# Narrow attention layer with two 64-row TensorE tiles, two-bank maxima and one key tile a step

## The reference

```
xn = rmsnorm(x, norm_w)                      # over 256 channels
q = (xn @ wq).reshape(B, T, 16, 16)          # T = 2048
k = (cond @ wk).reshape(B, S, 4, 16)         # S = 1601
v = (cond @ wv).reshape(B, S, 4, 16)
scores = einsum('btgrd,bsgd->bgrts', qg, k) / 4
attn = softmax(scores, axis=-1)
out = einsum('bgrts,bsgd->btgrd', attn, v)
return x + out @ wo
```

## Time and profile before

| | before |
|---|---|
| median of three timed executions | 4600.92 us |
| span of the profiled execution | 4597.9 us |
| TensorE busy | 4495.0 us, 98% |
| VectorE busy | 3081.4 us, 67% |
| ScalarE busy | 2309.8 us, 50% |
| mean granted TensorE clock | 0.987 |
| narrow layer's heads, end of head 0 to end of head 15 | 1742.24 to 2359.99 us |

### The profile page before, as it was taken

How to read it: one execution, slowest core, us unless ns; L and a number is a source line. 1 busy time by engine, 2 the same in 40 slices (tenths; PEclk the granted TensorE clock), 3 DMA queues, 4 the chain that set the end, 5 groups by cost and what they waited for, 6 DMA issues and landing times.

```text
span 4597.9 us, 56871 instructions
## 1 busy us (share of the span) xinstructions
PE 4495.0 (98%) x20657; PEld 2841.8 (62%) x20657; DVE 3081.4 (67%) x5037; ACT 2309.8 (50%) x4121; POOL 2827.0 (61%) x1365
## 2 busy tenths in 40 slices
PE   8999999999999979999999999999999999999999
PEld 7888866666656545555556666666656656665664
DVE  3321467777777678777846777777767677777776
ACT  3222455554555436666655555555555545554553
POOL 0000368898889711111036988898884888898886
PEclk9999999999999979999999999999999999999999
DMA  4555832221222021011234222222216212222220
GB/s 151 180 187 166 283 86 63 68 69 45 67 64 52 13 39 16 12 15 16 57 97 123 67 59 53 64 69 49 56 45 223 63 37 67 64 69 53 59 48 29
DMA packets 124633, 349.68 MB, mean 76 GB/s; under 512 B 28085, under 2 KB 46005, under 8 KB 113338
## 3 DMA queue, kind: packets, MB, share of 16 engines
q1 hardware_dynamic: 124352, 346.04, 28.4%
HBM read 191.31 MB, written 120.31 MB: 68 GB/s over the span
## 4 chain that ended last, share of the span: by engine, by line
PE 92%; DVE 6%; issue 1%; DMA 1%; ACT 0%; SPq 0%; POOL 0%; DVEq 0%; ACTq 0%
PE ST L989 13%; PE SS L970 12%; PE ST L990 12%; PE OA L1000 12%; PE OB L1000 11%; PE ST L1134 5%; PE OA L1142 4%; PE SS L1120 3%; DVE acc L1581 3%; PE OB L1120 1%; PE SS L1009 1%; DVE mpart L1560 1%; PE ST L1065 1%; PE ST L1066 1%; PE ST L1067 1%
## 5 line engine op out<-in xcount | busy, mean ns | idle before, releaser
L870 POOL TENSOR_TENSOR acc<-acc,P 128x1024 f32<-128x1024 f32 x912 | 2216.6, 2460 | 299.5 <-DVE acc L1587 286.3
L1321 ACT ACTIVATE P<-ST 128x512 f32<-128x512 f32 (+1 forms) x2496 | 1463.7, 597 | 1260.8 <-PE ST L990 1117.5
L1560 DVE TENSOR_REDUCE mpart<-SS 128x1 f32<-128x400 f32 (+1 forms) x3072 | 1629.7, 570 | 669.7 <-PE SS L970 594.4
L989 PE MATMUL ST<-QX,KX 128*128 128x512 f32 (+1 forms) x2496 | 1024.2, 410 | 3.5 <-DMA QS<-mrow 1.7
L970 PE MATMUL SS<-KS,QS 68*128 68x400 f32 (+1 forms) x3072 | 977.6, 352 | 14.7 <-DMA QS<-stq 8.3
L990 PE MATMUL ST<-QS,KS 69*128 69x512 f32 (+1 forms) x2496 | 990.1, 397 | 0.0
L970 PEld LDWEIGHTS SS<-KS,QS 68*128 68x128 f32 x3072 | 583.9, 190 | 191.3 <-DVE xacc L1611 23.9
L989 PEld LDWEIGHTS ST<-QX,KX 128*128 128x128 f32 (+1 forms) x2496 | 463.9, 186 | 360.2 <-issue 272.8
L1000 PE MATMUL OA<-P,Vp 128*64 128x512 f32 (+1 forms) x2496 | 658.3, 606 | 0.0
L1000 PE MATMUL OB<-P,Vp 128*64 128x512 f32 (+1 forms) x2496 | 641.3, 592 | 0.0
L1420 ACT ACTIVATE PG<-ST 128x512 f32<-128x512 f32 (+1 forms) x832 | 426.3, 618 | 213.3 <-PE ST L1134 213.1
(11 more groups left out here) (250 smaller groups left out, 4492.3 us busy)
## 6 DMA issues: line engine op xcount, KB each, us to landing
q_parts<-stq SPq DMA_DIRECT2D x96, 512.0 KB, 5.2
QX<-q_parts SPq DMA_DIRECT2D x96, 512.0 KB, 11.2
KX<-k_parts SPq DMA_DIRECT2D x48, 801.0 KB, 9.1
QS<-q_parts SPq DMA_DIRECT2D x45, 512.0 KB
R<-R SPq DMA_DIRECT2D x360, 64.0 KB, 2.0
v_tiles<-sv SPq DMA_DIRECT2D x24, 832.0 KB, 6.5
Vp<-v_tiles SPq DMA_DIRECT2D x24, 832.0 KB, 7.1
k_parts<-skh SPq DMA_DIRECT2D x48, 400.5 KB, 4.9
```

Of the source, the lines that this page charges most:

```text
L870: gp.tensor_tensor(out, out, P[0:k, slot(H, t), q, :], ALU.add).then_inc(pool_a, 1)
L989: pe.matmul(bank, KX[H % 2][:, t * 128:t * 128 + k], QX[H % 2][:, q], start=True, stop=False)
L1321: act.activation(P[0:k, slot(H, t), j, :], ST[n % 3][0:k, :], ACT.Exp, scale=SCALE).then_inc(act_p, 1)
L1560: dve.tensor_reduce(mpart[H % 2][:, i // len(KCH), c:c + 1], SS[RING_AT["s", H, i] % 3][:, 0:w], AX.X, ALU.max).then_inc(dve_ss, 1)
```

## The change

Only the narrow layer changes, and the names of four PSUM banks (SS0 to SS2 and OA become one tensor `S4` of four adjacent banks).

- Three parts of 16 rows are stacked in place of four of 32: K is (hi, hi, lo), Q is (hi, lo, hi), so the product lo times lo is left out. That makes 48 rows (49 with the max row), which fit in a 64-row tile of the array. K stands twice, at partitions 0 and 64. Q is divided: query blocks 0 and 2 at partition 0, blocks 1 and 3 at partition 64.
- `group_s` makes two matmuls for one item, one in each 64-row tile, into two adjacent banks; `group_s_max` reads both in one instruction. A head has 32 such pairs. The ring now has two places of two banks.
- `group_scores` with even j uses the lower tile, with odd j the upper.
- A step is one key tile: four ST matmuls, in two halves w = 0 and 1, each followed by one or two maxima pairs, then the PV of one tile. There are 13 steps a head.
- The output projection has four items of two banks instead of eight of one, and one add of 1024 columns for each; PV accumulates in OB.

```diff
-MROW = 3 * QD + D1
+GROWS = 3 * D1
+HALF = 64
+GPAIRS = SUNITS // 2
+HP = HU // 2
+GROW = KT - 3
+def group_units(h, t):
+    if t + 1 < KT:
+        return [(0, t + 1, j) for j in range(JQ)]
+    return [(1, 0, j) for j in range(JQ)] if h + 1 < HEADS else []
+def group_pairs(h, t, w):
+    if t >= GROW:
+        v = w + JQ // 2 * (t - GROW)
+        return 2, (part(GPAIRS, v, HP) if h + 2 < HEADS else range(0))
+    v = JQ // 2 * t + w
+    if h + 1 >= HEADS:
+        return 1, range(0)
+    return 1, (part(GPAIRS, v, JQ // 2 * GROW) if h == 0 else part(GPAIRS, HP - JQ // 2 * GROW + v, HP))
+def group_takes_row(h, t, w):
+    return t == GROW and w == 0 and h + 1 < HEADS
+def group_takes_sums(h, t):
+    return t == 3 and h > 0
+def group_o_item(h, t, w):
+    return t if h % GROUPS == 1 and h > GROUPS and t < JQ and w == 0 else None
+def group_q_item(h, t, w):
+    return t if h % QHEADS == QHEADS - 2 and h + 2 < HEADS and t < JQ and w == 0 else None
...
         def wait_group_ring(eng, at):
-            if at < len(GS):
+            if at < 2:
                 return
-            kind, n, i = GRING[at - len(GS)]
+            kind, n, i = GRING[at - 2]
...
             def group_q(h):
-                stack(GQ[h % 3], words(Q4hi[q, :]), words(Q4lo[q, :]), (0, 1, 0, 1), D1, gd_q[h % 3])
+                for i, src in enumerate((Q4hi, Q4lo, Q4hi)):
+                    blocks = words(src[q, :]).rearrange("d (b u c) -> d b u c", b=2, u=2)
+                    for half in range(2):
+                        to = HALF * half + i * D1
+                        sp.dma_start(words(GQ[h % 3][to:to + D1, 0:NQ // 2]).rearrange("d (b c) -> d b c", b=2),
+                                     blocks[:, :, half, :]).then_inc(gd_q[h % 3], 16)
...
             def group_s(h, i):
-                pe.matmul(GS[at % 4][:, 0:w], GQ[h % 3][0:MROW, qt * 128:(qt + 1) * 128],
-                          KG[h % GROUPS][0:MROW, o:o + w], start=True, stop=True).then_inc(gpe_s, 1)
+                for half in range(2):
+                    k = slice(HALF * half, HALF * half + GROWS)
+                    last = pe.matmul(group_bank("s", h, i, half)[:, 0:w], GQ[h % 3][k, qt * 128:(qt + 1) * 128],
+                                     KG[h % GROUPS][k, o:o + w], start=True, stop=True)
+                last.then_inc(gpe_s, 1)
...
             def group_scores(h, t, j):
                 wait(pe, gact_p, n - 2)
-                pe.matmul(ST[n % 3][0:k, :], KG[h % GROUPS][0:MROW + 1, t * 128:t * 128 + k],
-                          GQ[h % 3][0:MROW + 1, j * 512:(j + 1) * 512], start=True, stop=True).then_inc(gpe_st, 1)
+                r = slice(HALF * (j % 2), HALF * (j % 2) + GROWS + 1)
+                pe.matmul(ST[n % 3][0:k, :], KG[h % GROUPS][r, t * 128:t * 128 + k],
+                          GQ[h % 3][r, j // 2 * 512:(j // 2 + 1) * 512], start=True, stop=True).then_inc(gpe_st, 1)
...
             def group_head(h):
-                for g in range(STEPS):
-                    for u, (on, t, j) in enumerate(units(h, g)):
-                        group_scores(h + on, t, j)
+                for t in range(KT):
+                    both = group_units(h, t)
+                    for w in range(len(both) // 2):
+                        for on, ts, j in both[2 * w:2 * w + 2]:
+                            group_scores(h + on, ts, j)
...
                         for i in tiles:
                             group_s(h + ahead, i)
-                    pe.wait_ge(gact_p, HU * h + JQ * (PV[g][-1] + 1))
-                    for t in PV[g]:
-                        group_values(h, t)
+                    pe.wait_ge(gact_p, HU * h + JQ * (t + 1))
+                    group_values(h, t)
...
             def group_s_max(h, i):
-                dve.tensor_reduce(mpart[h % 2][:, i // len(KCH), c:c + 1], GS[GRING_AT["s", h, i] % 4][:, 0:w],
+                dve.tensor_reduce(mpart[h % 2][:, qt:qt + 9:8, c:c + 1], group_banks("s", h, i)[:, :, 0:w],
                                   AX.X, ALU.max).then_inc(gdve_ss, 1)
```

More of the change, by code:

```diff
@@ L351, in attention_layers @@
         ST = [bank(f"ST{i}") for i in range(3)]
-        SS = [bank(f"SS{i}") for i in range(3)]
-        OA, OB = bank("OA"), bank("OB")
+        S4 = ctx.enter_context(nc.psum_tensor("S4", [128, 4, 512], F32))
+        OB = bank("OB")
+        SS, OA = [S4[:, i, :] for i in range(3)], S4[:, 3, :]
         OAB = [OA, OB]
         PB = ST + SS + [OA, OB]
-        GS = SS + [OB]
         GB = [ST[0], ST[1], OA, OB]
@@ L885, in group_layer @@
                 for k in KG:
[L886 to L889, removed]
+                    for half in range(2):
+                        gp.memset(words(k[HALF * half + QD:HALF * half + 2 * QD, :]), 1.0).then_inc(pool_ones, 1)
                 for h in range(HEADS):
@@ L1109, in group_project @@
                 for ct in range(CT):
-                    last = pe.matmul(GS[at % 4][:, :], gwq[:, ct, :], xq[:, ct, j * 512:(j + 1) * 512],
+                    last = pe.matmul(group_bank("q", rnd, j), gwq[:, ct, :], xq[:, ct, j * 512:(j + 1) * 512],
                                      start=ct == 0, stop=ct == CT - 1)
@@ L1162, in group_head @@
[L1162 to L1172 removed]
+                pe.wait_ge(gpool_on, 4 * GROUPS * rnd + 4 * (GROUPS - 1) + j + 1)
@@ new lines, in group_output @@
+                wait_group_ring(pe, GRING_AT["o", rnd, j])
+                for ct in range(CT):
+                    last = pe.matmul(group_bank("o", rnd, j, ct), gwo[:, ct * 128:(ct + 1) * 128],
+                                     On[:, j * 512:(j + 1) * 512], start=True, stop=True)
+                last.then_inc(gpe_o, 1)
+            def group_head(h):
+                for t in range(KT):
+                    both = group_units(h, t)
+                    for w in range(len(both) // 2):
+                        for on, ts, j in both[2 * w:2 * w + 2]:
+                            group_scores(h + on, ts, j)
+                        ahead, tiles = group_pairs(h, t, w)
+                        if group_takes_row(h, t, w):
+                            group_transpose_max(h + 1)
+                        if group_o_item(h, t, w) is not None:
+                            group_output(h // GROUPS - 1, group_o_item(h, t, w))
+                        if group_q_item(h, t, w) is not None:
+                            group_project(h // QHEADS + 1, group_q_item(h, t, w))
@@ L1204, in group_layer @@
                 group_sums(HEADS - 1)
-                for i in range(8):
-                    group_output(ROUNDS - 1, i)
+                for j in range(JQ):
+                    group_output(ROUNDS - 1, j)
             for l in range(BIG):
@@ L1445, in group_layer @@
                     group_hi(0, j)
-                for t in PV[0]:
-                    for j in range(JQ):
-                        group_exps(0, t, j)
+                for j in range(JQ):
+                    group_exps(0, 0, j)
                 for h in range(HEADS):
@@ L1731, in group_layer @@
                     group_lo(0, j)
-                for i in range(SUNITS):
+                for i in range(GPAIRS):
                     group_s_max(0, i)
@@ L1738, in group_layer @@
                 group_reciprocals(HEADS - 1)
-                for i in range(8):
-                    group_add(ROUNDS - 1, i)
-                    if i % 2 == 1 and i > 1:
-                        split_x(1, (i - 3) // 2)
+                for j in range(JQ):
+                    group_add(ROUNDS - 1, j)
+                    if j > 0:
+                        split_x(1, j - 1)
             for l in range(BIG):
```

163 lines of the change are left out of this document (76 added, 87 removed).

## The result

Four timed executions of the changed kernel have a median of 4707.09 us (4692.26 to 4710.44), the kernel before beside them 4600.43. The ratio on record, taken over single executions, is 1.0224, 95% interval 1.0211 to 1.0237 (that of the two medians is 1.0232): slower by 107 us. The forecast was 4650, with a range that ended at 4696. The profiled execution took 4706.08 us.

What follows compares the result with a forecast made beforehand. A closed loop (first exponential, last score matmul, maxima work, PV, first score matmul) was taken to bound the kernel. Terms of 34 + 10 + 1 + 4 - 1 + 1 = 49 us gave 4650 us, range 4576 to 4696.

Steps and rivals of the forecast that it cites:

- plain-head term: Heads 1 to 13 and most of 14: a plain head takes 42.2 us instead of 39.74, +34 us.
- Thirteen loops: In a plain head, thirteen one-tile steps replace seven: 2.98 us each, three 0.19 longer, 39.3 us a head.
- Ring waits and max row: In plain heads, two-place ring waits add 0.9 and 0.3 us, the late negated maximum at tile 9 adds 0.46.
- The pair: Two 64-row maxima matmuls together cost one matmul of 0.19 us; the upper end adds 3.0 us a head.
- rival 1: The two row tiles or their loads do not overlap: 3.0 us a head on top, 4692 us; chance 0.17.
- Output items: Heads 5, 9 and 13: two-bank items hold up pairs in the ring, 3.4 to 3.6 us a head, +10 us.
- The query head: Head 6: its query items work like output items, 10.2 us against 9.2, +1 us.
- Head 15: Last head, without pairs: two one-tile steps take 5.36 us against 5.49, -1 us.
- Beginning: First maxima pass at 1.2 GHz, +3 us for 32 pairs, and the first head's Q loads, 1: together +4 us.
- Rival 2: In the steps: no ring waits, and half the output term, 4621 us; chance 0.12.
- Rival 3: The pair leaves the step's loop, running beside the last score matmul: step 2.79 us, 4578 us; chance 0.18.
- Rival 4: TensorE's work is the bound after all: 12.1 us a head vanish, 4420 us; chance 0.03.

Runs made afterwards that it cites:

- padded run: Changed kernel with each half's operands naming 63 rows (64 with the max row), Q's added rows zero, K's ones; 4626.34 us, 1.0056.
- full-row filler: Changed kernel with one additional score matmul over all 128 rows ahead of each tile's third; head 15 took 34.04 us, total not given.
- one and two repeats: Changed kernel with the third score matmul of each tile repeated once (4643.37 us, 1.0104) or twice (4626.70 us, 1.0054).
- the one with 48 rows alone: Kernel before with three parts of 16 rows, packed without gaps, in place of its four parts; 4796.52 us, 1.0426.

## Why the prediction was wrong in size

The direction and the mechanism of the step were right. That as much as half of the loss was forecast is luck: the sum put 49 us on what costs about 18, and nothing on what costs about 89. **The step that failed** is a term that is missing, the clock. The sum and all four rivals take every duration of the heads "at a granted clock of 1.00 (2.4 GHz)", read from the kernel before, and carry it over to operands of less than half the rows. Only the beginning was counted at 0.50. The padded run puts a least price on it: 107 - 27 = 80 us.

What the sum did hold, tested where the clock is mostly held (the padded run: +27 us, some 18 without its low stretches, where +49 was forecast). Nearly all of the difference is the plain-head term, 13.8 x 2.45 = 34 us forecast and 13.8 x 0.29 = 4 measured:

- *Thirteen loops.* Right as a mechanism, 0.14 too long: 2.84 us, not 2.98. The terms were good except one, the last score matmul, which starts 0.05 us after its bank is free where 0.26 was taken. 13 x 0.14 = 1.8 of the 2.2 us by which the plain head of 42.2 was over the measured 40.02.
- *Ring waits and max row.* Steps with three pairs are 0.31 longer, 3.15 us, close to the 3.28 and 3.27 worked out, and there are six of them as counted. The max row's step takes 3.00 (from 1868.85 to 1871.85), not 3.4.
- *The pair* costs one matmul, as taken; rival 1 is out. The maximum of two banks takes 0.99 us where 0.98 was worked out from the earlier trace rows.
- *Output items.* Right. In the padded run such a head is 10.15 us longer than a plain one, where it was 6.6 before: +3.55, and 3.4 to 3.6 was forecast. The query head is 10.6 longer where it was 9.2, so +1.4 for +1.
- *Head 15*: forecast -1. At full clock it took 34.0 us (with the full-row filler), the kernel before's 32.8 plus 1.2; with the low stretch of the padded run +7.8.
- *Beginning*: +1.4 at the end of head 0, for +4. Two other runs with the changed beginning end head 0 at 1739.01 and 1739.97 us (one and two repeats), before the 1742.24 of the kernel before, so no run shows the +4.

**Rivals.** Rival 2, no ring waits, 4621 us, is closest to what the arrangement alone costs (4626 measured, some 4618 by the estimate above), though for another reason: the waits are there, the base step is shorter. Rival 3 put the break-even step at 2.96 us; the measured mean is (7 x 2.84 + 6 x 3.15)/13 = 2.98, which is why a plain head at full clock is 0.3 us longer and no more. Rival 4, TensorE's work as the bound, is out: PE's busy time fell from 39.7 to 36.0 us a head, and the head did not get shorter. The pairs save TensorE work that nothing waited for: the loop runs through single latencies, and a pair's is the 0.35 us of one matmul.

The prediction's list of what could make it wrong named the switch between tiles of 64 rows and of 32 columns. That switch may be in the 0.60 us from the last score matmul to PV, where the sum had 0.23 + 0.29 = 0.52; a pair stands between, and no run separates the two.

What stays open: why the fall comes in some heads and not in others that have the same instructions (heads 3 and 4 of the changed kernel), and why 64 named rows in a half still leave a low stretch in heads 4, 14 and 15. No run tells how many rows are enough, or which part of the effect the ones in K have.

## What to carry to other kernels

Before operands are made shorter to fit a part of the array, read the granted clock in the stretches concerned, and keep it in the sum as a term of its own: an engine shown as wholly busy can run at half speed. Where rows are free, try naming them, with zeros in one operand and finite numbers in the other; it cost no time here and gave back 80 us in the changed kernel, 199 in the one with 48 rows alone. And halving an engine's work brings nothing where a closed loop of latencies sets the step: look for the order of that loop instead, which took a plain head to 39.3 us.

## What was not expected of the hardware

- TensorE at 1.2 GHz while shown busy for 74.12 of 74.12 us, with operands of 48 and 49 rows. The Trainium skill says in TensorE: Matmul & The Clock Gate, What's actually happening, that the clock is set by how busy TensorE has been lately. The busy time that the profile shows does not foretell the clock here: 224 matmuls a head in the same order are shown busy for all of a head at 0.82 with 48 rows and at 1.00 with 127.
- Rows that add nothing to the result kept the clock up: of the 127 rows, 79 held zeros in Q and ones in K, and the clock was 1.00 where it was 0.82 without them.
- A half-clock stretch nearly doubles what TensorE does in it (PV from 1.06 to 1.93 us), but a head of 40 us of the changed kernel grows only to 58 to 61; four exponentials take 2.08 to 2.12 us in it, where they took 2.06.
